# A graph-attention and mixture-of-experts kernel: filler products moved on TensorE, and an expert loop without a written-out rest

## The reference, cut to what matters

```python
h = layernorm(x) @ W                      # 8192 x 256
e = leaky_relu((h @ a1)[:, None] + (h @ a2)[None, :])
e = where(adj > 0, e, -9e15)              # adj: 8192 x 8192 int32, 268 MB
x = x + elu(softmax(e, axis=1) @ h)
xf = layernorm(x)
idx = argmax(xf @ router_w.T + router_b)  # one of 32 experts a token
y = relu(relu(xf @ W1[idx] + b1[idx]) @ W2[idx] + b2[idx])
out = x + y
```

## Time and profile before

| | us |
|---|---|
| median of three runs | 1067.19 |
| lowest, highest | 1064.69, 1069.18 |
| the profiled execution's own time | 1062.02 |
| its span in the trace | 1060.3 |
| mean granted TensorE clock, share of full speed | 0.915 |

### The profile page before, as it was taken

The page is one execution under the profiler, slowest core; times in us unless marked ns, Lnnn a source line. Parts: engine busy times, 40 slices in busy tenths (PEclk is TensorE's granted clock), DMA queues, the critical chain, the costliest instruction groups (busy, mean ns, idle before and its releaser), DMA issues.

```text
span 1060.3 us, 25495 instructions
## 1 busy us (share of the span) xinstructions
PE 885.5 (84%) x4456; PEld 609.8 (58%) x4524; DVE 758.0 (71%) x4010; ACT 786.9 (74%) x1339; POOL 683.2 (64%) x766
## 2 busy tenths in 40 slices
PE   5989488898989988898988898898898957388994
PEld 4767255565655655565655565555565646266773
DVE  5878267787778877787877787777787864455663
ACT  2656678898979988988988988898898811166663
POOL 3778366666767766766766766677676764156664
PEclk9999689988989998989998989899999976599998
DMA  9998979999999999999999999999999993155551
GB/s 344 396 381 285 367 270 410 401 374 411 394 415 398 416 388 405 397 382 413 408 397 409 396 398 413 399 392 413 415 385 412 296 241 103 42 162 164 169 168 48
DMA packets 84778, 357.32 MB, mean 337 GB/s; under 512 B 26070, under 2 KB 52655, under 8 KB 68353
## 3 DMA queue, kind: packets, MB, share of 16 engines
q1 hardware_dynamic: 56226, 296.78, 72.8%
q0 software_dynamic: 27776, 60.06, 15.8%
q10 hardware_dynamic: 736, 0.05, 0.0%
HBM read 343.67 MB, written 32.05 MB: 354 GB/s over the span
## 4 chain that ended last, share of the span: by engine, by line
PE 30%; DMA 27%; issue 19%; POOL 14%; DVE 8%; POOLq 1%; ACT 0%; DVEq 0%; ACTq 0%
DMA G_all<-wh_table,idx 23%; POOL G_all L614 12%; PE psO L1661 8%; PE psW L1577 6%; PE psO L1798 3%; PE psF L1595 2%; PE psO L1586 2%; DMA out_x<-raw_all,tok 1%; PE psL L1787 1%; PE psO L1663 1%; PE psW L1787 1%; DMA wh_table<-mean_sb 1%; PE psO L1568 1%; POOL out_x L690 1%; PE psT L1671 1%
## 5 line engine op out<-in xcount | busy, mean ns | idle before, releaser
L614 POOL DMA_INDIRECT G_all<-wh_table,idx x384 | 411.2, 1071 | 224.7 <-issue 128.7
L737 ACT ACTIVATE sg<-raw_all,minus_tiny 128x1024 fp8e4<-128x1024 int32 x256 | 311.5, 1217 | 3.5 <-DMA raw_all<-in_adj 3.1
L740 ACT ACTIVATE sg<-raw_all,minus_half 128x1024 fp8e4<-128x1024 int32 x256 | 313.5, 1225 | 0.0
L1661 PE MATMUL psO<-G_all,diag 128*128 128x256 f32 x640 | 190.5, 455 | 16.2 <-DVE diag L1161 16.2
L1586 PE MATMUL psO<-word_no,share 128*128 128x512 bf16 x826 | 199.0, 381 | 3.1
L1661 PEld LDWEIGHTS psO<-G_all,diag 128*128 128x128 f32 x640 | 140.9, 229 | 42.0 <-issue 19.3
L1586 PEld LDWEIGHTS psO<-word_no,share 128*128 128x128 bf16 x885 | 87.7, 104 | 90.9 <-issue 1.1
L1595 PE MATMUL psF<-sg,fold_w 128*128 128x512 bf16 x512 | 135.6, 388 | 0.0
L900 DVE MAX8 top_word<-psF 128x8 f32<-128x256 f32 x256 | 108.1, 425 | 12.9 <-issue 10.7
L690 POOL DMA_INDIRECT out_x<-raw_all,tok x81 | 78.9, 974 | 59.5 <-DVE raw_all L1517 30.7
L644 POOL DMA_INDIRECT regions<-x,posu x64 | 67.8, 1059 | 42.1 <-issue 24.3
(11 more groups left out here) (224 smaller groups left out, 1890.9 us busy)
## 6 DMA issues: line engine op xcount, KB each, us to landing
raw_all<-in_adj SPq DMA_DIRECT2D x128, 2048.0 KB
raw_all<-regions SPq DMA_DIRECT2D x84, 130.0 KB, 2.1
wh_table<-G_all POOLq DMA_DIRECT2D x16, 520.0 KB, 9.2
x_sb<-in_x SPq DMA_DIRECT2D x8, 1024.0 KB, 16.9
G_all<-wh_table,idx POOLq DMA_INDIRECT x384
regions<-pad_row SPq DMA_DIRECT2D x32, 130.0 KB
x_sb<-in_L_ffn_W SPq DMA_DIRECT2D x4, 512.0 KB
x_sb<-in_L_ffn_W SPq DMA_DIRECT2D x8, 256.0 KB
```

What stands on the lines that cost most here:

```text
L614: pool.indirect_dma_start(out=G[par][:, k, :], out_offset=None, in_=table[:, :], in_offset=bass.IndirectOffsetOnAxis(ap=idx[par][:, k:k + ...
L737: act.activation(sign_of[par][q][0], raw_of[b][q % 2][0], ACT.Identity, bias=minus_tiny[:, 0:1], scale=TINY, saturate=False)
L740: act.activation(sign_of[par][q][1], raw_of[b][q % 2][1], ACT.Sign, bias=minus_half[:, 0:1], saturate=False).then_inc(a_sg, 1)
L1661: pe.matmul(psO[par][:, 0:D], diag[:, k, :], G[par][:, k, 0:D], start=(k == 0), stop=False)
```

## The change

Four things are changed.

1. In `step` on TensorE, the four filler products between the first fold and `tail_scores` now stand behind the second fold and `tail_ends`, directly ahead of `ranks`. Their condition is now `do.attend`, so that steps 59 to 63 have them too.
2. The filler at a step's end is issued for every step with `do.fetch` (u < 63): nine as before up to step 58, five in steps 59 to 62. With the four of point 1 that is nine a step in the last steps.
3. `blocks_loop` has no written-out rest. The loop of turns goes to nine in place of seven; a turn beyond `steps` is skipped by its condition. The load of `steps` into a register stands behind the first twelve block steps on every engine, where before it stood ahead of them. GpSimd waits for the plan and loads the count of stores (`rows_out`) ahead of the blocks, and no longer behind them.
4. `turn_of` is summed over nine turns, and two bounds in the assertion are widened.

```diff
@@ blocks_loop
-        TURNS = BLOCKS // RING
+        TURNS = -(-(BLOCKS + TAIL) // RING)
...
-                    if not isinstance(i, int) or 0 <= i - lag < BLOCKS:
+                    if not isinstance(i, int) or i >= lag:
                         stage(i - lag, (r - lag) % RING, turn if lag <= r else turn - 1)
             eng.wait_ge(v_plan, PLAN_STEPS)
             eng.nop(nofuse=True)
-            steps = eng.value_load(steps_i[0:1, 0:1], min_val=1, max_val=BLOCKS + TAIL)
             for r in range(RING):
                 step(r, r, 0)
+            steps = eng.value_load(steps_i[0:1, 0:1], min_val=1, max_val=BLOCKS + TAIL)
             with eng.Fori(1, TURNS) as turn:
                 with eng.If(steps > turn * RING):
                     for r in range(RING):
                         step(turn * RING + r, r, turn)
-            with eng.If(steps > TURNS * RING):
-                for i in range(TURNS * RING, BLOCKS + TAIL):
-                    step(i, i % RING, i // RING)
-            return steps
@@ gpsimd
-            steps = blocks_loop(pool, [(store_block, TAIL)])
-
-            with pool.If(steps > TURNS * RING):
-                for k in range(STORES):
-                    pool.wait_ge(y_out[k], 16 * ((BLOCKS + STORES - 1 - k) // STORES))
-                    pool.nop(nofuse=True)
-            with pool.If(steps < TURNS * RING + 1):
-                rows_out = pool.value_load(steps_i[0:1, 1:2], min_val=16, max_val=16 * BLOCKS)
-                for k in range(STORES):
-                    pool.wait_ge(y_out[k], rows_out)
-                    pool.nop(nofuse=True)
+            pool.wait_ge(v_plan, PLAN_STEPS)
+            pool.nop(nofuse=True)
+            rows_out = pool.value_load(steps_i[0:1, 1:2], min_val=16, max_val=16 * TURNS * RING // STORES)
+            blocks_loop(pool, [(store_block, TAIL)])
+            for k in range(STORES):
+                pool.wait_ge(y_out[k], rows_out)
+                pool.nop(nofuse=True)
@@ tensor, step
                 if do.search:
                     fold(u + LAG, par, 0)
-                if do.ahead:
-                    keep_busy(u, par, 4)
                 if do.attend:
                     tail_scores(u, par)
                 if do.search:
                     fold(u + LAG, par, 1)
                 if do.prepare:
                     tail_ends(u + 2)
+                if do.attend:
+                    keep_busy(u, par, 4)
                 if do.place:
                     ranks(u - 2)
...
-                if do.ahead:
-                    keep_busy(u + 1, 1 - par, 9)
+                if do.fetch:
+                    keep_busy(u + 1, 1 - par, 9 if do.ahead else 5)
```

More of the change, by code:

```diff
@@ L59, in gat_moe @@
     NULL_ROW = E // 2 * SPAN
-    assert RING % STORES == 0 and RING % 2 == 0 and TAIL % STORES == 0 and 2 * GROUP >= GROUP + GATHERS and BLOCKS // RING <= E and LAG % 2 == 0 and NS % (2 * GROUP) == 0 and NS >= LAG + 4 and 3 * RING <= BLOCKS <= P
+    assert RING % STORES == 0 and RING % 2 == 0 and TAIL % STORES == 0 and 2 * GROUP >= GROUP + GATHERS and -(-(BLOCKS + TAIL) // RING) <= E and LAG % 2 == 0 and NS % (2 * GROUP) == 0 and NS >= LAG + 4 and 3 * RING <= BLOCKS and -(-(BLOCKS + TAIL) // RING) * RING <= P
     ctx = ExitStack()
```

## The result

| | before | after |
|---|---|---|
| median of 20 runs each, us | 1067.27 | 1060.36 |
| lowest, highest | 1058.50, 1077.86 | 1056.45, 1075.75 |
| ratio, 95 % interval | | 0.9949 (0.9929 to 0.9969) |
| profiled execution's span | 1060.3 | 1055.2 |
| its mean granted TensorE clock | 0.915 | 0.927 |

The change makes the kernel 0.51 % faster, 5.4 us by the ratio with 2.1 either way (the medians differ by 6.9). The forecast said 11.8 us. The direction was right and the time lies inside the range, but by the ratio less than half of the forecast gain is there.

What follows compares the result with a forecast made beforehand. The prediction saw loads leaving little room (DMA share 0.99 to 1.01) and lowered TensorE clock lengthening weighted sums. Its terms, 7 + 4.5 + 0.3 = 11.8 us off the 1067.2 median, gave 1055.4 us, range 1045 to 1070.

Steps and rivals of the forecast that it cites:

- The ceiling of 24 us: Middle 53 steps: the most a full clock can give back, 619.0 us instead of 642.86, 23.8 less.
- Part 1: Steps 0 to 58: four products ahead of `ranks` hold clock for weighted sum; 7 us off, bounds 24 and -13.
- three tenths of the ceiling: Middle steps: expected share of the clock loss won back, 0.3 x 23.8 = 7 us.
- The promised clock of 0.96: Stretch from 190 to 830 us: mean granted clock should rise from 0.94 to 0.96 or more.
- Part 2: Steps 59 to 63: nine products a step bring sums of 62 and 63 to full clock; 4.5 us off.
- Part 3: Block loop: first block starts earlier as a register load moves behind it; 0.3 us gained, bounds 1 and -3.
- D: Block loop: skipped turns stall GpSimd and other engines by code fetches, two times 1.7 us; 1058.8 us, chance 0.07.
- My test for it, over 11 us: End of the span: more than 11 us behind the last store would show code-fetch stalls, rival D.
- C: Longer emptiness before `tail_scores` lowers the clock in more steps, weighted sum included; slower, 1077.7 us, chance 0.13.
- B: Steps are held by DMA, and only the last ones gain; 1062.4 us, chance 0.15.
- E: Fill does nothing to the clock on balance, falls only change place, last steps included; 1066.9 us, chance 0.13.

Runs made afterwards that it cites:

- point 1 alone: Kernel before with the four filler products moved ahead of `ranks`, in steps 0 to 58 only: 1062.24 us, ratio 0.9943.
- point 2 alone: Kernel before with four products ahead of `ranks` and five at the step's end, steps 59 to 63 only: 1067.95 us (1.0006), again 1068.93 us (0.9980).
- The slow last steps: Changed kernel with twelve more products directly ahead of the weighted sum in steps 59 to 63: 1067.64 us, ratio 0.9969.
- the fastest version: Changed kernel plus six products ahead of `tail_scores`, also in steps 59 to 63, and nine at the end of steps 59 to 62: 1053.66 us, 0.9850.

## Why the prediction was half right

**What bounds the kernel.** The reading of the rows holds, and its last sentence on them (the loads leave little room below) deserved more weight than it got in the sum. The ceiling of 24 us came from the four fastest steps, whose length I put down to the clock alone. With the clock nearly full throughout, the stretch is 631 to 637 us long, not 619: what made those four steps short was more than the clock, and what it was isn't shown.

**Part 1, forecast -7 us.** Right in mechanism, and in size partly by luck. The chain of causes is seen link by link in step 30: longer wait, earlier fall, second fold slow and without a hole, clock back for the sum. The late wait was to grow by 0.9 us; the mean of those over 0.3 us goes from 1.48 to 2.42. The idle time ahead of `ranks` was to be near zero: 13.3 us in all became 0.0. The size: 0.9943, -6.1 us, with 3.7 either way. But "three tenths of the ceiling" had no working behind it, and two errors cancel in it: the sums became shorter by 17.5 us (21 with point 1 alone), some three quarters or more of the ceiling, and only about a third of that reached the time. The promised clock of 0.96 is there with point 1 alone and not in the trace of the whole change (0.94); step lengths of 12.0 us likewise (12.04 against 12.18).

**Part 2, forecast -4.5 us.** This is the step that failed. I had the chain go through the sums of 61, 62 and 63, took those of 62 and 63 at full speed, 5.0 us off the path, and let all of it reach the end. Measured is 1.0 us with 2.2 either way, so 4.5 lies outside. The sums did become faster: in the changed kernel those of steps 59 to 63 take 2.8, 4.8, 4.4, 4.1 and 2.8 us where before had 4.5, 4.9, 5.3, 5.4 and 5.5, together 6.7 us less. (I had 62 at full clock and it was not; I had 60 as no gain.) But in the steps that wait for gathered rows part of it comes back as a longer wait, and in that wait the clock falls again. Step 62 of the kernel with point 2 alone, in its second group of runs, shows it, TensorE, with the clock of the two stretches behind the wait:

```profile
878.11 1.24 PE L1586 MATMUL psO<-word_no,share 128*128 128x512 bf16 x5
884.78 0.57 PE L1647 MATMUL psW<-slot_s,to_row 128*128 128x11 f32 x2 [5.43 <-DVE slot_s L1123]
...
888.39 4.61 PE L1661 MATMUL psO<-G_all,diag 128*128 128x256 f32 x10
```

```profile
884.00:886.00 2.00, 1.22 (x4) 0.71 (x5) 1.21 (x11) 0.00 (x0) 1.66 (x2) 0.50 1.09 325
886.00:888.00 2.00, 2.00 (x9) 1.09 (x8) 1.60 (x9) 0.40 (x2) 1.42 (x2) 0.50 0.99 242
```

The wait ahead of step 62 was 1.54 us and is 5.43; the sum takes as long as before. Why the wait grew is in GpSimd's timeline and in the chain that ended last:

```profile
870.85 1.07 POOL L614 DMA_INDIRECT G_all<-wh_table,idx  x1 [2.53 <-PE psO L1663]
```

```profile
877.66 6.67 DMA G_all<-wh_table,idx
884.36 0.29 DVE slot_s L1123
```

The gather for step 62 starts when step 60's sum has ended (870.06), since that sum frees its buffer. GpSimd issues its six DMAs one behind the other up to 877.66, and the last lands 6.67 us later. Step 61's sum ran at the full clock, took 2.8 us and ended at 877.68, and nothing in this chain waited for it: its gain became idle time. The path leads from sum 60 over a gather to sum 62, past sum 61. In the changed kernel it is the same (step 60's sum ends at 868.4, the gather for 62 lands at 882.5). What is left of the gain in this trace is mainly the sum of 63, 2.8 us in place of 5.5.

Measured from the issue of the last adjacency load to the end of the last sum, the kernels with point 2 and full loads have 70.5 to 71.8 us (72.9 where the sums up to step 58 were slowed) and those without 73.2 to 76.4: 3 us of the 6.7 are left. This loss is shown. The executions have -1.0 us, but 3 lies inside their interval (2.2 either way), so a second loss behind it is not shown. The slow last steps have such a gap too (11 us in the trace, 2 by the ratios, 7 by the medians), and it stays open.

**Part 3, forecast -0.3 us.** The start is as forecast: between `plan_i` and SyncE's first issue lie 1.17 us (1.73 before), and nothing stands in the way behind it.

```profile
915.04 0.28 DVE L1442 TENSOR_SCALAR plan_i<-psL 1x128 int32<-1x128 f32 x1
```

```profile
916.49 3.79 SPq L512 DMA_DIRECT2D raw_all<-regions  x4
```

The rest is below what can be measured (1.0005, with 0.37 % either way).

**The rivals.** D didn't happen. The last store of the changed kernel is issued at 1043.60, 11.6 us ahead of the end of the span at 1055.2, as before (1048.65 to 1060.3):

```profile
1043.60 0.97 POOL L686 DMA_INDIRECT out_x<-raw_all,tok  x1 [0.39 <-issue]
```

My test for it, over 11 us, was badly put, since before itself is over 11; by its own comparison the answer is plain. So the rule of the Trainium skill (Runtime: NRT & Kernel Launch, Instruction fetch mechanics) on taken branches has no price that shows behind two skipped turns. Whether a stall is hidden in the landing of the last store no run shows. C's fall of the clock in the longer wait is real, but it ends before the sum, and fewer sums are slow, 5 against 15. B, the steps held by DMA with a gain in the last ones alone, 1062.4 us, is nearest in time by the ratio (D, 1058.8, by the median) and wrong in both halves of where: the gain is in the middle, and the last steps give almost none. Its argument, that a sum that ends sooner meets a gather that is as late, is nevertheless what the traces show for a part of the rest. E is refuted by point 1 alone.

In short: 7 forecast and 6 measured for point 1, 4.5 forecast and 1 measured for point 2, 0.3 and 0 for the blocks. Together that would be 7 us; the whole change shows 5.4 with 2.1 either way.

## What to carry to other kernels

In a loop that also waits for transfers, time taken off one engine's path need not reach the end: here about a third of it did, and in the last steps the rest turned up as a longer wait one step later, in which TensorE fell back to its low clock. Before pricing such a gain, look in the trace at who is released by the faster instruction and whether that one already waits for a DMA. Here, with two gather buffers in turn, the sum of step 60 released the gather for 62, and the one between them counted for nothing in that chain. In this kernel filler paid most when every hole had some, the long wait too: adding products there as well gave 16 us where moving four gave 5.

## What the runs showed of the hardware

- With the same program the mean granted clock alone does not fix the time: six executions of the fastest version, all at 0.961 to 0.967, run from 1050.7 to 1060.3 us.
- One chip ran the kernel before in 1269 us, 19 % longer than the others. The changed kernel without point 2 had 2.7 us stops of VectorE there in 40 of 53 steps at one place and 321 GB/s, where the traces of other chips have about 400. No trace of the kernel before was kept on that chip. The same edit (four more products ahead of `tail_scores`) was worth 1.4 % (0.7 to 2.1) on one chip and 6.1 % on this one.
- In the last steps the last of the six gather DMAs of step 62 landed 6.67 us after its issue (point 2 alone, second time).
- In the changed kernel's step 30 TensorE was empty for 2.85 us, ran at 1.2 GHz from 499, and was back at 2.4 GHz in the microsecond from 502, with work and no hole between. Here the hole that cost the clock did the weighted sum no harm, since 4.7 us of other work, without an idle moment, stood between the two.
